# Expert biases as three bfloat16 parts, opened in the tilings of the matmuls beside them

## The reference, cut to what matters

```python
grouped = x.reshape(b, s // g, g, d)                  # groups of 32 tokens
logits = einsum('bntd,des->bntes', grouped, Wc) + bc + tie
perm = (logits == max(logits, axis=-3, keepdims=True))  # each of 128 experts picks a token
permuted = einsum('bntd,bntes->bnesd', grouped, perm)
inner = relu(einsum('bnesd,esdf->bnesf', permuted, W1) + b1)   # 512 -> 32
result_permuted = einsum('bnesf,esdf->bnesd', inner, W2) + b2  # 32 -> 512
result = einsum('bnesd,bntes->bntd', result_permuted, perm)
```

## Time and profile before

| what | value |
|---|---|
| three runs, us | 1740.51, 1743.48, 1747.41 |
| median, us | 1743.48 |
| span of the profiled execution, us | 1740.2 |
| its own time beside the span | not given |
| TensorE busy, share of the span | 93% |
| VectorE, ScalarE, GpSimd busy | 75%, 42%, 49% |
| records: matmuls, weight loads | 22,488 each |
| granted TensorE clock, mean | 0.988 |

### The profile page before, as it was taken

One profiled execution on the slowest core, in us unless ns is written; L12 is line 12 of the kernel. 1 busy time (PEld: TensorE's weight loads), 2 busy tenths in 40 slices (PEclk: granted clock), 3 DMA queues, 4 the chain that ended last, 5 costly groups with the idle time before them and its releaser, 6 DMA issues.

```text
span 1740.2 us, 51861 instructions
## 1 busy us (share of the span) xinstructions
PE 1626.6 (93%) x22488; PEld 1141.0 (66%) x22488; DVE 1297.2 (75%) x1890; ACT 734.0 (42%) x961; POOL 858.5 (49%) x1020
## 2 busy tenths in 40 slices
PE   8899999999999999999889899999999988999995
PEld 4677777777777777777676555566455666555662
DVE  5777777777777777777748777777777877777766
ACT  3533223333323232333235555555555554555552
POOL 3467777887787778777731233122233122223122
PEclk9999999999999999999999999999999999999997
DMA  7635544554555454545565888777888877888776
GB/s 277 176 100 162 187 132 169 161 165 153 160 180 166 152 157 157 185 133 180 157 220 167 213 218 219 222 202 196 216 226 215 230 209 198 228 210 217 218 177 157
DMA packets 180498, 324.81 MB, mean 187 GB/s; under 512 B 23088, under 2 KB 33200, under 8 KB 178864
## 3 DMA queue, kind: packets, MB, share of 16 engines
q1 hardware_dynamic: 135008, 238.63, 43.6%
q0 software_dynamic: 17616, 32.52, 11.5%
q10 hardware_dynamic: 27648, 50.34, 9.0%
HBM read 242.71 MB, written 78.71 MB: 185 GB/s over the span
## 4 chain that ended last, share of the span: by engine, by line
PE 63%; DMA 13%; DVE 12%; issue 5%; ACT 3%; POOL 2%; SPq 1%; ACTq 1%; POOLq 0%; DVEq 0%
PE ps L1463 12%; PE ps L919 11%; PE ps L966 10%; PE ps L1436 7%; PE ps L979 5%; PE ps L1487 4%; DMA xin<-out 4%; PE ps L934 3%; DMA gat<-in_W 3%; DMA out<-xin 3%; PE ps L992 3%; DVE mx L709 2%; PE ps L1502 2%; DMA sel<-lg_scratch 2%; PE ps L1482 2%
## 5 line engine op out<-in xcount | busy, mean ns | idle before, releaser
L182 POOL TENSOR_SCALAR xin<-xin,r_all,nb_all 128x512 f32<-128x512 f32 x128 | 116.3, 912 | 522.0 <-DMA xin<-out 380.0
L1362 DVE STREAM_TRANSPOSE res<-res 128x2048 f32<-128x2048 f32 x128 | 292.1, 2296 | 0.1
L1311 ACT ACTIVATE gat<-ps 128x1536 f32<-128x1536 f32 (+1 forms) x128 | 171.2, 1344 | 227.4 <-PE ps L1436 227.3
L919 PE MATMUL ps<-xTh,qh 128*128 128x512 f32 x512 | 209.3, 409 | 5.1 <-DVE qs L726 1.4
L1378 DVE COPY res<-ps 128x1024 f32<-128x1024 f32 x128 | 156.7, 1224 | 65.8 <-PE ps L1487 65.8
L919 PE MATMUL ps<-xTh,ql 128*128 128x512 f32 x512 | 200.6, 392 | 0.0
L919 PE MATMUL ps<-xTl,qh 128*128 128x512 f32 x512 | 199.6, 390 | 0.0
L1436 PE MATMUL ps<-sel,xin 32*128 32x128 f32 x4096 | 157.5, 283 | 43.5 <-issue 21.2
L1368 DVE COPY gat<-ps 128x512 f32<-128x512 f32 (+1 forms) x128 | 103.9, 816 | 95.2 <-PE ps L1436 94.4
L1436 PEld LDWEIGHTS ps<-sel,xin 32*128 32x128 f32 x4096 | 132.5, 186 | 59.3 <-issue 30.7
L1282 POOL DMA_DIRECT2D out<-xin x120 | 122.6, 1114 | 90.4 <-DVE xin L1198 76.5
(11 more groups left out here) (161 smaller groups left out, 3320.0 us busy)
## 6 DMA issues: line engine op xcount, KB each, us to landing
gat<-in_W ACTq DMA_DIRECT2D x192, 256.0 KB, 5.5
xT<-in_xT SPq DMA_DIRECT2D x32, 1024.0 KB, 6.1
xin<-in_x SPq DMA_DIRECT2D x64, 512.0 KB, 3.8
out<-xin SPq DMA_DIRECT2D x64, 512.0 KB, 3.9
xin<-out SPq DMA_DIRECT2D x128, 256.0 KB, 4.1
xin<-in_W SPq DMA_DIRECT2D x128, 256.0 KB, 3.9
out<-xin POOLq DMA_DIRECT2D x120, 256.0 KB, 7.3
xT<-in_W SPq DMA_DIRECT2D x68, 256.0 KB, 4.5
```

Of the source, the lines that this page charges most:

```text
L182: e.tensor_scalar(self.xn[:, t, :], self.xn[:, t, :], self.r[:, i, t:t + 1], self.nb[:, i, t:t + 1], ALU.mult, ALU.add).then_inc(self.m_xn ...
L919: last = e.matmul(ps[:, 2 + n % 2, :], a[:, c, n * DH:(n + 1) * DH], b[:, c, :], start=(k == 0), stop=(k == len(parts) - 1))
L1311: e.activation(o, v, ACT.Copy).then_inc(m_gaA.sem, 1)
L1362: e.transpose(v, v).then_inc(m_tr.sem, 1)
```

## The change

Both biases are kept as three bfloat16 parts, whose sum is the float32 value to within the third rounding. In each row group of 32, rows 0 to 7 hold the first part, 8 to 15 the second, 16 to 23 the third, and 24 to 31 zero (a row per expert of the group). `rowk` has, for each of eight experts, ones in that expert's three rows. It is made once, in the preparation, instead of in the first batch.

- `outer`: the four float32r matmuls 32x512 in 32x128 tiles become 16 bfloat16 matmuls 32x512 in 32x32 tiles, the tiling and order of the 16 float32 ones behind them.
- `bias`: the four float32 matmuls (eight records) become four bfloat16 ones, in 32x128 tiles as before.
- waits for the constants stand at the first batch only.
- preparation: the parts are formed by ScalarE (round), VectorE (rest of rows 8 to 31), ScalarE (round), VectorE (rest of rows 16 to 23), for three tiles: b2's first half, b1, b2's second half (1,024, 128 and 1,024 columns). The third goes through its steps within the first attention unit. b2's second half has a DMA of its own, into the room of `lt`; b1 is one DMA in place of four. Host data for them is three times stacked.

```diff
-        b1r = sb0("b1r", [P, P])
-        b2s = sb0("b2s", [P, 2, D], F32R)
-        part = sb0("part", [P, 18])
+        with nc.sbuf_tensor("owc", [P, 2, D], F32R) as owc:
+            pass
+        b2s = sb0("b2s", [P, 4, D], BF16)
+        b1s = sb0("b1s", [P, P], BF16)
+        part = sb0("part", [P, 10])
+        rowk = sb0("rowk", [P, 8, NG], BF16)
...
-            e.dma_start(b2w[:], b2_dram).then_inc(d_b2.sem, 16)
+            e.dma_start(bias_parts[0][0], b2_dram[:, 0:2]).then_inc(d_bias.sem, 16)
+            e.dma_start(bias_parts[1][0], b1_dram).then_inc(d_bias.sem, 16)
+            e.wait_ge(m_kvs.sem, m_kvs.at(0, C - 1))
+            e.dma_start(bias_parts[2][0], b2_dram[:, 2:4]).then_inc(d_bias.sem, 16)
...
-            e.activation(b2s[:], b2w[:], ACT.Copy).then_inc(m_b2h.sem, 1)
+            def bias_first(k):
+                w, o = bias_parts[k]
+                e.wait_ge(d_bias.sem, d_bias.at(0, 2))
+                e.activation(o, w, ACT.Copy).then_inc(m_b2h.sem, 1)
+
+            def bias_second(k):
+                w, o = bias_parts[k]
+                e.wait_ge(m_b2l.sem, m_b2l.at(0, k))
+                e.activation(o, w, ACT.Copy).then_inc(m_b2c.sem, 1)
...
+            for k in range(3):
+                bias_first(k)
+            e.activation(rowk[:], part[:, 0:8].unsqueeze(2).broadcast_to([P, 8, NG]), ACT.Copy).then_inc(m_row.sem, 1)
+            bias_second(0)
+            bias_second(1)
...
+                if g == -1:
+                    bias_second(2)
...
-            e.tensor_tensor(b2t[:], b2w[:], b2s[:].bitcast(F32), ALU.subtract).then_inc(m_b2l.sem, 1)
-            e.tensor_scalar(b2t[:], b2t[:], part[:, 17:18], None, ALU.mult).then_inc(m_b2l.sem, 1)
-            e.scalar_tensor_tensor(out=b2s[:], in0=b2s[:].bitcast(F32), scalar=part[:, 16:17], in1=b2t[:],
-                                   op0=ALU.mult, op1=ALU.add).then_inc(m_b2s.sem, 1)
+            def bias_rest(k):
+                w, o = bias_parts[k]
+                e.wait_ge(m_b2h.sem, m_b2h.at(0, k))
+                e.scalar_tensor_tensor(out=w, in0=o, scalar=part[:, 8:9], in1=w, op0=ALU.mult, op1=ALU.add).then_inc(m_b2l.sem, 1)
+
+            def bias_last(k):
+                w, o = bias_parts[k]
+                e.wait_ge(m_b2c.sem, m_b2c.at(0, k))
+                e.scalar_tensor_tensor(out=o, in0=o, scalar=part[:, 9:10], in1=w, op0=ALU.mult, op1=ALU.add).then_inc(m_b2s.sem, 1)
+
+            bias_rest(0)
+            bias_rest(1)
+            bias_last(0)
+            bias_last(1)
...
                 if unit(g + 1):
                     turned(g + 1, 0)
                     turned(g + 1, 1)
+                if g == -1:
+                    bias_rest(2)
...
                 if unit(g + 1):
                     turned(g + 1, 2)
+                if g == -1:
+                    bias_last(2)
...
-                    e.matmul(ps[:, s, :].rearrange("p (q n) -> p q n", q=8), b1r[r, :],
-                             ident[r, s * G + 8 * s:s * G + 8 * s + 8].unsqueeze(2).broadcast_to([G, 8, 2 * NG]),
+                    e.matmul(ps[:, s, :].rearrange("p (q n) -> p q n", q=8), b1s[r, :],
+                             rowk[r, :, 0:1].broadcast_to([G, 8, 2 * NG]),
                              start=True, stop=False, skip_group_check=True)
...
-                e.wait_ge(m_b2s.sem, m_b2s.at(0))
-                e.wait_ge(m_row.sem, m_row.at(0))
-                for j in range(4):
-                    r = slice(j * F, (j + 1) * F)
-                    e.matmul(ps[:, bank(u) + j, :], rowk[r, u // 2, :], b2s[r, u % 2, :],
-                             start=True, stop=False, skip_group_check=True)
+                if i == 0 and u == 0:
+                    e.wait_ge(m_b2s.sem, m_b2s.at(0, 2))
+                for k in range(4):
+                    for j in range(4):
+                        r = slice(j * F, (j + 1) * F)
+                        e.matmul(ps[k * NG:(k + 1) * NG, bank(u) + j, :], rowk[r, u % 2 * 4 + k, :], b2s[r, u // 2, :],
+                                 start=True, stop=False, skip_group_check=True)
```

More of the change, by code:

```diff
@@ L90, in build @@
         bcol = sb0("bcol", [P, 1])
-        b1r = sb0("b1r", [P, P])
-        b2s = sb0("b2s", [P, 2, D], F32R)
-        part = sb0("part", [P, 18])
+        with nc.sbuf_tensor("owc", [P, 2, D], F32R) as owc:
[4 more added lines that the diff above has]
+        rowk = sb0("rowk", [P, 8, NG], BF16)
         tie = sb0("tie", [P, G])
-        consts = (bcol, b1r, b2s, part, tie)
+        consts = (bcol, b1s, b2s, part, rowk, tie)
         const_loads = [(bcol, bc), (tie, tie_in.partition_broadcast(P)), (part, part_in)]
-        const_loads += [(b1r[s * Q:(s + 1) * Q], b1) for s in range(4)]
         xin = sb0("xin", [P, RING, TH, D])
@@ L288, in attention @@
         vcs = xin[:, 2:4].rearrange("p u n d -> p (u n) d")
-        owc = [b2s[:, k, :] for k in range(2)]
+        owc = [owc_room[:, k, :] for k in range(2)]
         first_bank = lambda k: (4, 6)[k] if k < 2 else (4, 6, 2)[(k - 2) % 3]
@@ L1102, in experts @@
         NY = TH
-        bcol, b1r, b2s, part, tie = consts
+        bcol, b1s, b2s, part, rowk, tie = consts
         xn = route.xn
@@ L1558 @@
     w2 = np.asarray(L0_ffn_W2).reshape(4, 8, 4, D, F).transpose(1, 2, 4, 0, 3).reshape(8, P, UW)
-    b1 = np.asarray(L0_ffn_b1).reshape(Q, P)
-    b2 = np.asarray(L0_ffn_b2).reshape(4, 4, 2, 4, D).transpose(3, 1, 0, 2, 4)
-    b2 = np.stack([b2, b2], axis=2).reshape(P, 2, D)
-    row = np.arange(F)
-    part = np.zeros((4, F, 18), np.float32)
-    part[:, row, row // 8 * 4 + row % 4] = 1.0
-    part[:, row, 16 + row // 4 % 2] = 1.0
-    part = part.reshape(P, 18)
+    thrice = lambda v: np.concatenate([v, v, v, np.zeros_like(v)], axis=1).reshape(P, *v.shape[2:])
+    b1 = thrice(np.asarray(L0_ffn_b1).reshape(4, 8, P))
+    b2 = thrice(np.asarray(L0_ffn_b2).reshape(4, 4, 2, 4, D).transpose(3, 2, 0, 1, 4).reshape(4, 8, 4, D))
+    row = np.arange(24)
+    part = np.zeros((4, F, 10), np.float32)
+    part[:, row, row % 8] = 1.0
+    part[:, 8:24, 8] = -1.0
+    part[:, 16:24, 9] = -1.0
+    part = part.reshape(P, 10)
     qa, qb = np.asarray(L0_xattn_q_w)[:, :, :DH // 2], np.asarray(L0_xattn_q_w)[:, :, DH // 2:]
```

45 lines of the change are left out of this document (20 added, 25 removed).

## The result

The changed kernel took 1765.49 us, the median of 4 runs (1757.20 to 1775.57); the kernel before, run beside it, 1745.15 us (1740.51 to 1747.41). The ratio is 1.0132, with a 95% interval of 1.0095 to 1.0170: slower by 1.3% (the two medians alone are 1.2% apart), where 1732 us and a range up to 1750 were forecast. The profiled execution has a time of its own of 1765.78 us and a span of 1764.0, 23.8 us more than the span before; its mean granted clock is 0.989, where it was 0.988.

What follows compares the result with a forecast made beforehand. Each expert-half batch was taken as two pieces in series: TensorE paces second gather to scatter, the DMA chain scatter to second gather. 1740.2 - 6.2 - 6.3 + 0.9 = 1728.6; with 3.3, 1732 us, range 1708 to 1750.

Steps and rivals of the forecast that it cites:

- the rival on the other side: Instruction fetching gets worse, at the gathers after L1446: 1747 us at 1 us a batch more; chance 0.15.
- the wait for L182: Second gather (L1436) waiting for GpSimd: absorbs the second layer's gain in most batches, rising from 4.8 to 25 us or more.
- the second layer as lying off the path in twelve batches: Scatter to second gather: the DMA chain, some 23.6 us, sets the pace, so second-layer savings there give nothing.
- The packets more: Instruction queue: 12 packets more in all; in the second layer one is used up in 3.3 us instead of 4.4.
- The second layer's unit: From some 1.57 to 1.29 us, bound by VectorE's copies; 2.2 us off a stretch of eight, 6.2 us in sum.
- The first layer's opening: L1446 from 1.07 to 0.44 us; at most 0.38 a batch comes through, 6.3 us in sum.
- The preparation: Once, at the start: the biases' steps on ScalarE and VectorE make L725 and TensorE start 0.9 us later.
- a sum of 1732: Whole kernel: span 1740.2 - 6.2 - 6.3 + 0.9 = 1728.6, with 3.3 us added for the median.
- if a unit stays at 1.5: Second layer, sign of being wrong: a unit stays at 1.5 us instead of about 1.29.
- if the gaps without a wait change by more than 15 us: TensorE's idle gaps with no wait shown, sign of being wrong: they change by more than 15 us.

Runs made afterwards that it cites:

- the kernel with four matmuls: Changed kernel, but four bfloat16 matmuls 32x512 in 32x128 tiles open each second-layer unit instead of 16; 1728.14 us, 0.9923 of the kernel before.
- the cut W2 loads: W2 loads in the batches cut to 64 of 512 columns: four matmuls a unit 1690.98 us, kernel before 1704.47, changed kernel 1731.96.
- the shifted kernel before: Kernel before plus 32 one-column float32 matmuls (128 records, half a packet) once before the first batch's first second-layer unit; 1727.42 us, ratio 0.9924.
- the one run that tried to join them: Four bfloat16 matmuls a unit, plus eight one-column pairs a batch and 64 once, holding packet edges at the shifted places; 1733.54 us, ratio 0.9975.

## Why the prediction was wrong

**The mechanism was named, and put in the wrong place at a wrong price.** The step that failed is that of the rival on the other side: "What is lost there vanishes in the wait for L182; what is lost between L1446 and the scatter counts." For a shorter second layer it was right: with four matmuls a stretch is 0.6 us shorter, scatter to second gather only 0.2 (23.72 for 23.92), and the wait for L184 rises from 4.8 to 7.7 us. For a longer one it can't be. All waits of L1436 for L182 together are 4.8 us, 0.3 us a batch, and that is all that a longer stretch can vanish in. The stretches grew by 25.3 us, and scatter to second gather by 1.20 us a batch. The step behind it was to treat the second layer as lying off the path in twelve batches, from the chain of one and waits that were tenths of a microsecond long. One batch earlier in the chain of the same trace it lies on the path:

```profile
1066.09 2.79 PE ps L1502 x23
1069.32 1.07 PE ps L1487 x32
1070.82 1.07 PE ps L1487 x32
1072.42 1.07 PE ps L1487 x32
```

The two paths, second layer and DMA chain, were in most batches within some tenths of a microsecond of each other, so a change to either had to be priced in both directions.

**The packets more were entered at nothing in the sum.** The prediction had 12 more (the queue shows 11) and the rate at which they are used up, "while DMA is full". It left them to a rival of 1 us a batch with a chance of 0.15. Its reading of the rate was wrong where it mattered: it has 3.3 us for a packet in the second layer "instead of 4.4", but 72 records a unit at 1.57 us make some 5.6 us before, which the trace shows (5.64), against 4.10 after. The packets were ready in 5.4 us. So the kernel before lay just on the safe side, and the change went over. What the runs show in its place: with four matmuls in a unit, 36 pairs, a second-layer stretch is 12.53 us in the mean; with 48 pairs it is 14.72 or 14.73, whether the twelve that are added carry 512 columns or one. That is 2.2 us a stretch, 35 us in all, of the 37 us between 1728.14 and 1765.49.

**The second layer's unit was sized by the wrong bound.** The forecast was a unit of 1.29 us and 2.2 us off a stretch (from 1.57 as "the mean of both"; the mean of 1.51 and 1.58 is 1.55). The cost of the opening was right (0.23 us for 0.24), and a unit by itself comes 1.09 us after the last (1132.85 to 1133.94). But the pace is not two copies of 1.29 us in a row. It is the loop in the chain above: a unit's own length, VectorE's copy, and the unit after next. A loop takes 2.98 us (1132.85 to 1135.83), 1.49 a unit, where it took 3.09 (1015.98 to 1019.07 in the trace before). An undisturbed stretch went from 12.57 to 11.95 us with four matmuls: 0.6 us instead of 2.2. The wait for L182, of which at least 25 us were forecast, is 2.5 us.

**The first layer's opening was right; what it is worth was not shown alone.** L1476's successor follows after 0.33 us (forecast 0.44, before 1.07). Of the kernel with four matmuls and the cut W2 loads, 13.5 us under the kernel before with that cut, the second layer's 16 stretches explain 6.6 us by their means or 9.9 by their shortest, and the preparation costs 1.2; what remains for the first layer is 8.1 or 4.8 us, where 6.3 were forecast. It was not run alone: by the pieces of a batch that kernel gains 0.85 us from opening to scatter (23.80 for 24.65), 12 us in 14 batches, but there the places of the edges have changed too. In the changed kernel itself the opening's gain is lost again at edges in the products: opening to scatter is 25.66 us for 25.74.

**The preparation was nearly right.** 0.9 us was forecast; at the first layer's first opening the kernel is 1.2 us late. VectorE near the start, after:

```profile
66.82 1.29 DVE L869 SCALAR_TENSOR_TENSOR pr<-b2s,part,pr 128x1024 f32<-128x1024 bf16 x1 [1.51 <-ACT b2s L676]
68.02 0.35 DVE L869 SCALAR_TENSOR_TENSOR b1w<-b1s,part,b1w 128x128 f32<-128x128 bf16 x1
69.23 1.28 DVE L874 SCALAR_TENSOR_TENSOR b2s<-b2s,part,pr 128x1024 bf16<-128x1024 bf16 x1 [0.86 <-ACT b2s L681]
70.43 0.34 DVE L874 SCALAR_TENSOR_TENSOR b1s<-b1s,part,b1w 128x128 bf16<-128x128 bf16 x1
70.81 0.69 DVE L746 TENSOR_TENSOR qc<-ps,cos 128x512 f32<-128x512 f32 x1
```

The heads' first step is at 70.81, and was at 69.81; 0.3 us of this was there before the biases' steps began (ScalarE's first copy starts at 65.74, before at 65.46).

**What stays right of the forecast** is the kernel with four matmuls: 1728 us, for a sum of 1732. That is luck as a sum: by the pieces above its gain of 1.10 us a batch is 1.06 from opening to scatter, where 0.38 was forecast, and the stretch gave 0.6 for 2.2. Of the conditions for being wrong, two came true. One is "if a unit stays at 1.5": 1.49 a unit in the loop above, and 1.84 as the mean of all. The other is "if the gaps without a wait change by more than 15 us". On the lines of the groups above they went from 35.4 us to 64.3 (gather 6.8, products 35.7, second layer 21.8), 28.9 us more.

**What is open.** What a given place of the edges costs can't be foretold from these runs: half a packet of shift gave the kernel before 13 us, all of it ahead of the scatter, and the same places gave nothing in a kernel with four matmuls. Why a packet starts so late behind an edge while the DMA engines are full, whether it stands in their queues or for another cause, no run shows. Best of all were the kernel with four matmuls and the shifted kernel before, 0.9923 and 0.9924; their gains did not add up in the one run that tried to join them (0.9975).

## What to carry to other kernels

Instructions come by the DMA engines: where TensorE issues many short matmuls, work out in how many microseconds 256 records are used up, and set it beside the DMA share of the same stretch. Here 5.6 us were just enough with full engines and 4.1 were not; sixteen matmuls in place of four opened a unit 0.2 us faster and cost a stretch of eight units some 2 us in packets that came late. A wait that absorbs a gain absorbs a loss only up to its own length, so when two paths end within tenths of each other, price both signs. And a gap that the profile ends with "issue", in the middle of a group of like matmuls, is to be numbered in records from the start, the sequencer's waits among them: if such gaps share a remainder by 256, it is the fetching, and the packets' own times can confirm it.

## What was not expected of the hardware

- Twelve one-column matmuls in front of each unit, 1,536 in the kernel, cost 35.8 us (1763.89 against 1728.14), 23 ns each, for 12 columns a unit.
- 32 one-column matmuls more (128 records), executed once, made the kernel before 13 us faster (0.9924): its packets' edges had moved by half a packet.
- 16 bfloat16 matmuls 32x512 in 32x32 tiles took 0.23 us from the first one's start to that of the next group; their own starts lie within 0.05 us, 3 ns apart. The Trainium skill (TensorE: Matmul & The Clock Gate, Wait — 56ns, not 53.3ns?) has about 25 ns as the least distance of two starts. By that they would take 0.40 us, an estimate; in this tiling the trace doesn't agree.
- All of TensorE's records come as 3.11 MB, 0.7% of the DMA engines' time. It is not their amount that hurts, nor the transfer of a packet (about 1 us in either state), but that it starts late: in the second layer 3.27 us behind the edge before with full engines, 1.39 us with half-free ones.
